# Local attention's softmax sums, taken from ScalarE's exponentials to a VectorE reduction one round later

## The reference

```python
sim = jnp.einsum('bhwid,bhwjd->bhwij', bq, bk)
mask = (i < j) | (i > j + WINDOW) | (j == -1)
sim = jnp.where(mask, -jnp.finfo(sim.dtype).max, sim)
attn = jax.nn.softmax(sim, axis=-1)
out = jnp.einsum('bhwij,bhwjd->bhwid', attn, bv)
```

## Time and profile before

| | |
|---|---|
| median of 3 runs | 4749.59 us |
| the profiled execution | 4749.3 us, its span (first to last instruction) 4747.2 us |
| TensorE busy | 3981.9 us (84%) |
| VectorE busy | 2996.4 us (63%), 5727 instructions |
| ScalarE busy | 2767.4 us (58%), 6174 instructions |
| GpSimd busy | 2068.3 us (44%) |
| mean granted TensorE clock | 0.943 of full speed |

### The profile page before, as it was taken

The page is one execution under the profiler, slowest core; times in us unless marked ns, Lnnn a source line. Parts: engine busy times, 40 slices in busy tenths (PEclk is TensorE's granted clock), DMA queues, the critical chain, the costliest instruction groups (busy, mean ns, idle before and its releaser), DMA issues. The chain is left out here.

```text
span 4747.2 us, 54512 instructions
## 1 busy us (share of the span) xinstructions
PE 3981.9 (84%) x17140; PEld 2417.0 (51%) x17140; DVE 2996.4 (63%) x5727; ACT 2767.4 (58%) x6174; POOL 2068.3 (44%) x1349
## 2 busy tenths in 40 slices
PE   6888898888888888888987989878888888888877
PEld 4446554555445554455544555445554555545423
DVE  4436657666576674766657666666757666576564
ACT  3566557555576555665665655756557555575432
POOL 2213345444264441753436435454435444265344
PEclk9998999999999999999999999999999999999889
DMA  3020013111131111210121101311113111131122
GB/s 105 5 87 1 26 47 125 35 40 44 39 120 40 36 50 63 87 53 26 59 90 59 53 30 56 110 39 52 33 43 125 35 40 44 39 118 48 49 80 81
DMA packets 188825, 274.03 MB, mean 58 GB/s; under 512 B 23448, under 2 KB 102900, under 8 KB 188532
## 3 DMA queue, kind: packets, MB, share of 16 engines
q1 hardware_dynamic: 186340, 268.72, 17.6%
q10 hardware_dynamic: 2192, 1.70, 0.1%
HBM read 215.54 MB, written 54.79 MB: 57 GB/s over the span
## 5 line engine op out<-in xcount | busy, mean ns | idle before, releaser
L621 POOL TENSOR_TENSOR work<-work 128x512 f32<-128x512 f32 x512 | 666.9, 1303 | 1216.5 <-DVE work L681 1129.0
L1545 POOL TENSOR_TENSOR work<-work,minus_half 128x8 f32<-128x8 f32 x256 | 473.7, 1864 | 542.5 <-DVE work L1528 539.4
L681 DVE SCALAR_TENSOR_TENSOR work<-work,psum 128x512 f32<-128x512 f32 x528 | 362.0, 686 | 420.3 <-ACT work L613 419.5
L1648 ACT ACTIVATE work<-psum,work 128x128 f32<-128x128 f32 (+1 forms) x1024 | 391.5, 396 | 385.6 <-DVE work L1670 385.2
L589 PE MATMUL psum<-work,w_up 128*128 128x512 f32 x1024 | 546.0, 616 | 64.3 <-DVE work L681 60.4
L613 ACT ACTIVATE work<-psum 128x512 f32<-128x512 f32 x528 | 315.4, 598 | 434.1 <-PE psum L589 427.1
L595 PE MATMUL psum<-work,w_down 128*128 128x512 f32 x1024 | 541.7, 612 | 3.3 <-POOL work L621 3.3
L1473 PE MATMUL psum<-wqkv,xn 128*128 128x512 f32 x768 | 389.4, 634 | 56.1 <-PEq L404 39.4
L1613 PEld LDWEIGHTS psum<-work 128*128 128x128 f32 x3072 | 392.4, 199 | 61.6 <-issue 48.4
L1613 PE MATMUL psum<-work 128*128 128x64 f32 x3072 | 415.5, 280 | 9.2 <-ACT work L1635 8.6
L1602 PE MATMUL psum<-ident,work 128*128 128x128 f32 x1536 | 250.4, 288 | 147.0 <-ACT work L1648 112.5
(11 more groups left out here) (237 smaller groups left out, 8501.8 us busy)
## 6 DMA issues: line engine op xcount, KB each, us to landing
work<-expert_weight_rows SPq DMA_DIRECT2D x1024, 128.0 KB, 2.9
position_scores<-work SPq DMA_DIRECT2D x64, 768.0 KB, 3.5
work<-position_scores SPq DMA_DIRECT2D x64, 512.0 KB, 3.8
work<-state_readout_rows SPq DMA_DIRECT2D x72, 256.0 KB, 4.3
rows<-state_readout_rows SPq DMA_DIRECT2D x32, 256.0 KB, 3.9
sq<-state_readout_rows SPq DMA_DIRECT2D x24, 256.0 KB, 4.2
rows<-in_L_attn_q SPq DMA_DIRECT2D x8, 256.0 KB, 3.6
expert_weight_rows<-work SPq DMA_DIRECT2D x16, 128.0 KB, 2.3
```

Source lines behind the costliest of these rows:

```text
L621: pool.tensor_tensor(h, h, self.weights[p % self.SLOTS], ALU.mult).then_inc(self.gated, 1)
L681: v.scalar_tensor_tensor(out=self.gate_h[p % 3][0:rows], in0=self.tanh_h[p % self.turns][0:rows], scalar=1.0, in1=bank(b, self.ups[p % sel ...
L1545: pool.tensor_tensor(half, half, b.minus_half[:].broadcast_to([128, LH]), ALU.pow).then_inc(self.inv_norm, 1)
L1648: ins = self.nc.scalar.activation(out[:, x, -n:] if t else out[:, x], self.scores(m)[:, x], ACT.Exp, bias=self.neg_max[i % 2][:, slot:slot ...
```

## The change

ScalarE's exponentials lose `accum_out`. A new VectorE function, `totals`, adds up a group's probabilities with one `tensor_reduce` out of SBUF: 512 elements in each partition, into 4 sums for groups 0 and 1 and into 2 for groups 2 to 5. It stands in round m + 1, behind the copy and the maxima of that round and ahead of everything else there. Each pass has 6 of them, so there are 384 in all. A new semaphore, `totalled`, lets ScalarE overwrite a tile of probabilities only when it has been added up, and lets `scale_heads` read the sums only when they are there.

```diff
@@ exps
         if t and m >= 4:
             act.wait_ge(self.p_turned, group - 1)
+            act.wait_ge(self.totalled, group - 1)
         elif i >= 1:
             act.wait_ge(self.p_turned, group - (3 if t else 5))
+            act.wait_ge(self.totalled, group - (3 if t else 5))
...
-                                            bias=self.neg_max[i % 2][:, slot:slot + 1], accum_out=self.sums[i % 2][:, at:at + 1])
+                                            bias=self.neg_max[i % 2][:, slot:slot + 1])
...
+    def totals(self, dve, i, m):
+        t, heads, _ = self.group(m)
+        group, first = self.GROUPS * i + m, 8 * t + heads[0]
+        dve.wait_ge(self.exped, group + 1)
+        self.nc.vector.tensor_reduce(self.sums[i % 2][:, first:first + 2 * len(heads) - 1:2],
+                                     self.probs_of(m).rearrange("p (h k) -> p h k", h=len(heads)), AX, ALU.add).then_inc(self.totalled, 1)
...
     def scale_heads(self, dve, i, t):
+        dve.wait_ge(self.totalled, self.GROUPS * i + (2, 6)[t])
         dve.wait_ge(self.o_ready, self.GROUPS * i + (2, 6)[t])
...
@@ attend_vector, after the copy and the maxima of the round
+            if m < self.GROUPS:
+                self.totals(dve, i, m)
             if m == 2:
                 self.scale_heads(dve, i, 0)
```

More of the change, by code:

```diff
@@ L1443, in __init__ @@
         self.o_t = carve(4 * SEQ).rearrange("p (j n) -> p j n", j=4)
+        self.totalled = sem("exps_totalled")
         self.lens, self.neg_max, self.sums = two(16), two(16), two(16)
@@ L1642, in exps @@
             act.wait_ge(self.p_turned, group - 1)
+            act.wait_ge(self.totalled, group - 1)
         elif i >= 1:
             act.wait_ge(self.p_turned, group - (3 if t else 5))
+            act.wait_ge(self.totalled, group - (3 if t else 5))
         out = self.probs_of(m).rearrange("p (h k) -> p h k", h=len(heads))
         for x, head in enumerate(heads):
-            at, slot = 8 * t + head, 8 * t + self.slot(m) + x
+            slot = 8 * t + self.slot(m) + x
             ins = self.nc.scalar.activation(out[:, x, -n:] if t else out[:, x], self.scores(m)[:, x], ACT.Exp,
-                                            bias=self.neg_max[i % 2][:, slot:slot + 1], accum_out=self.sums[i % 2][:, at:at + 1])
+                                            bias=self.neg_max[i % 2][:, slot:slot + 1])
         ins.then_inc(self.exped, 1)
```

## The result

The changed kernel takes 4793.0 us (median of 6 runs, 4781.2 to 4802.5), the kernel before 4747.7 us (6 runs beside it, 4742.5 to 4750.0). The ratio is 1.0091, 95% interval 1.0073 to 1.0109: slower by 0.9%. 4782 us was forecast. The profiled execution of the changed kernel took 4790.5 us, its span 4788.4 us, mean granted clock 0.939 (before: 4749.3, 4747.2 and 0.943).

What follows compares the result with a forecast made beforehand. TensorE was taken to be bound by waits for ScalarE's exponentials and VectorE's gate. Terms of 19.6 + 8.2 + 9.4 - 4.5 = 32.7 us on 4749.3 us gave 4782 us, range 4752 to 4820.

Steps and rivals of the forecast that it cites:

- The prices of the instructions: VectorE and ScalarE: 685 ns for a sum, 0.61 us in a full queue; exponentials 1.18 us for four heads, 0.74 for two.
- some 42 us of sums less 9 us of exponentials: Whole kernel: the split the prediction gave for its 32.7 us of added time.
- L589 has no slack there: Pass 2, round 5: the sum of group 4 stands ahead of the gate, +1.38 us, and TensorE's up product takes it all.
- the sum of group 3 disappears in: Pass 2, round 4: GpSimd's chain comes 0.77 us later, the stalled rotary work ends with it and hides this sum.
- The forecast of 1.4 us: Pass 2 with experts: each longer by 1.4 us, 14 times, 19.6 us.
- Rival D: Passes 2 and 0 of "third" stages: stalls hide more, costing 0.6 us each instead of 1.4 and 1.1; 4767 us, chance 0.12.
- the sums of groups 1 and 3 would be free: Passes 0 and 2: by the skill's contention rule alone, tensor_reduce never contends with GpSimd, so these sums cost nothing.
- Pass 0 of "third" stages: Three sums enter VectorE's full queue, less idle time and exponentials' gain: 1.09 us six times, 1.66 once, 8.2 us.
- rival C: Passes 0 and 2: longer idle drops TensorE's clock 20 more times at 1.44 us, 29 us more; 4811 us, chance 0.20.
- "First" stages: Passes 0 and 1: sums ahead of routing and gate, less idle time and exponentials' gain, 1.34 us, 7 times: 9.4 us.
- The added waits: Semaphore waits for the sums: cost nothing visible, since what the sums wait for was computed a round before.
- The exponentials' gain: ScalarE without accumulator reads: 0.32 us for groups 0 and 1, 0.17 us for groups 2 to 5, where on the path.

Runs made afterwards that it cites:

- e8: Changed kernel, but in passes 0 and 2 VectorE sums only groups 4 and 5, the others keep `accum_out`; 4742.3 us, 0.9977 of the kernel before.
- e7: Changed kernel, but in passes 0 and 2 VectorE sums only groups 1 and 3, the others keep `accum_out`; 4762.0 us, 1.0024 of the kernel before.
- e10: Changed kernel with eight matmuls without use on TensorE in round 3 of pass 2, ahead of the gate; 4791.3 us, 1.0087 of the kernel before.
- e5: Changed kernel with each sum of passes 0 and 2 at the end of its round, behind gate or routing step; 4900.3 us, 1.0312 of the kernel before.
- e1: Kernel before with the 384 VectorE sums added into an unread tile and `accum_out` kept; 4835.4 us, 1.0187 of the kernel before.
- e2: Changed kernel without the VectorE sums, the inverted sums a constant 1, so neither sums nor accumulation; 4720.9 us, 0.9938 of the kernel before.

## Why the prediction was right, and where it was not

- **The prices of the instructions** were right: 677 ns for a sum (685), 1.14 and 0.73 us for the exponentials (1.18 and 0.74), and in a full queue a sum steps by 0.59 us, as in the rows of stage 4 (0.61).
- **The place of the loss** was right: passes 0 and 2, pass 1 of "third" stages unchanged to 0.01 us, pass 3 shorter by 0.36 us (0.32 forecast). The wait for the gate was to grow by 15 to 20 us; it grew by 26.8.
- **The sum** came out near, 4782 for 4793 us, in part by luck: its terms missed by up to 8 us each, in both directions. Its sentence "some 42 us of sums less 9 us of exponentials" doesn't follow from its terms, which make 48 less 15.
- **The step that failed is pass 2**, "L589 has no slack there" and "the sum of group 3 disappears in" the stalled rotary work. Both were read from one stage in which the clock falls. In the other seven passes L589 had 0.6 us of slack, which makes the sum ahead of the gate free (e8), and the short rotary instructions weren't stalled until the sums moved them onto GpSimd's work (the rows of stage 4; e7 has the cost without the other sums). The stall was taken as a thing into which a sum could disappear; at full clock the sum brought it about. The forecast of 1.4 us held in six of the seven passes where the clock had fallen before (1.21 us; 0.68 in the seventh) and not in the other seven (2.4 to 2.9 us). Rival D, the stalls hiding more, went the wrong way for the same reason. So did the inference that the sums of groups 1 and 3 would be free because GpSimd doesn't slow them: they took 665 to 687 ns everywhere, but what stood behind them was slowed.
- **Pass 0 of "third" stages**: the mechanism was right (round 5 was 0.94 us late, 1.09 forecast), the size too small by a second low stretch of the clock, 2.6 us in all. This is rival C in part. Its 20 more passes with a fall didn't come: four more of the passes 2 and six more of these passes have one. Nor is a fall at one price: in pass 2 it costs 1.70 us before (32.37 against 30.67), 0.53 changed (33.58 against 33.05) and nothing in e10 a round later, where rival C had 1.44.
- **"First" stages** were to cost 9.4 us and cost 1.7. Pass 0 lost 8.3 us in sum, but pass 1 gained 6.6: in four of the seven it went from 34.2 us at a clock of 0.95 to 32.45 at 1.00. That was in no term.
- **The added waits** cost nothing, as said, but for a narrower reason than was given (e5).
- **The exponentials' gain**: e1 against the changed kernel makes it 42 us when the sums are there (26 at one clock), e2 against the kernel before 27 us when they are not, against 15 us in the terms of the prediction. A kernel in which VectorE and ScalarE take turns in being late gives no single price for either.

What stays open: why the clock falls in a given pass and not in its twin. Stages 7 and 8 of the kernel before have pass 2 alike in every start and duration up to 17.2 us, with the same wait of 1.62 us for the gate, and the clock falls in the one only. And how much of the loss in pass 2 is the stall alone: no run takes it away and leaves VectorE as late as it is.

## What to carry to other kernels

Before you charge or spare a moved instruction, look at the same place in several repetitions of the loop, one at full clock and one at the lower level: slack and stalls differ between them. Ask of work that is pushed later not only who waits for it, but on what other engine's instruction it will now lie; here the reductions, themselves not slowed by GpSimd, pushed instructions that are. And a reduction that reads a tile becomes the owner of that tile: its place in the queue sets when the next writer may start, which cost more here (e5) than all the sums did where the change puts them.

## What the runs showed of the hardware

- VectorE's 256-column TENSOR_TENSOR out of SBUF takes 0.41 us alone and 1.26 to 1.50 us when it starts behind GpSimd's 512-column TENSOR_TENSOR; its 512-column ones 0.69 and 1.65. One that started 0.01 us ahead of GpSimd's (stage 8 before, 2338.46) took 0.41 us. The added TENSOR_REDUCE took 665 to 687 ns in all 384 places, many of them beside GpSimd's work. The Trainium skill, "SBUF — State Buffer", section "Who interferes with whom", says that a VectorE instruction with two SBUF inputs contends with GpSimd's reads and that a tensor_reduce on trn2 never does; the trace agrees.
- The accumulator read is long in the records (207 ns) and short on the path: without it a step of four heads is 0.36 us shorter, 0.09 us for each.
- The run-to-run spread follows the clock. Over all runs of these kernels, with a level of its own for each kernel, a mean granted clock lower by 0.001 goes with about 3 us more time, and what is left scatters by 2 to 7 us. At a clock of 0.942 the changed kernel would be at 4783 and the kernel before at 4750: of the 45 us between the medians some 12 are more time at the lower level.
- Filling TensorE's idle time ahead of one fall of the clock moved it to a later gap, 6 us on in eight passes and 13 in three (e10).
